# Layer 1 of two fused attention layers in two phases: raw scores kept in SBUF with a running maximum

## The reference

```python
# layer 0: 64 inner channels, no scale
f = einsum('bni,bim->bnm', theta_x, phi_x)
y = einsum('bnm,bmi->bni', softmax(f), g_x)
x = W_w @ y + W_b + x
# layer 1: 128 channels, scale 1/sqrt(128)
attn = softmax(einsum('bnc,bcm->bnm', q, k) * scale)
x = x + einsum('bnm,bmc->bnc', attn, v)
```

## Time and profile before

| | |
|---|---|
| median of three runs | 3430.94 us (3430.82 to 3434.11) |
| the profiled execution | 3435.51 us, its span 3433.7 us, mean granted clock 0.989 |
| busy, share of the span | PE 97%, POOL 86%, DVE 61%, ACT 49% |
| a steady block of layer 0 | 44.0 us |
| a steady block of layer 1 | 59.9 us |

### The profile page before, as it was taken

How to read it: one execution, slowest core, us unless ns; L and a number is a source line. 1 busy time by engine, 2 the same in 40 slices (tenths; PEclk the granted TensorE clock), 3 DMA queues, 4 the chain that set the end, 5 groups by cost and what they waited for, 6 DMA issues and landing times.

```text
span 3433.7 us, 46684 instructions
## 1 busy us (share of the span) xinstructions
PE 3336.5 (97%) x13124; PEld 2113.4 (62%) x13124; DVE 2100.6 (61%) x3029; ACT 1671.5 (49%) x2241; POOL 2965.9 (86%) x1366
## 2 busy tenths in 40 slices
PE   6999999999999989999999998999999999999998
PEld 4555566666655556666655555666665555566665
DVE  4555576776555557676755555677675555666674
ACT  4455445444455544444445554544454555444444
POOL 4999699898989969898989996989898999688897
PEclk9999999999999999999999999999999999999999
DMA  1000000000000000000000000000000000000000
GB/s 43 13 18 19 28 10 22 12 22 16 19 19 16 19 23 16 16 19 19 13 19 19 19 16 23 19 13 21 16 19 13 19 19 16 19 13 16 13 13 10
DMA packets 34038, 61.73 MB, mean 18 GB/s; under 512 B 5280, under 2 KB 5920, under 8 KB 33568
## 3 DMA queue, kind: packets, MB, share of 16 engines
q1 hardware_dynamic: 33824, 59.23, 5.6%
HBM read 42.44 MB, written 16.78 MB: 17 GB/s over the span
## 4 chain that ended last, share of the span: by engine, by line
PE 91%; DVE 3%; issue 2%; POOL 2%; ACT 1%; SPq 0%; DVEq 0%; DMA 0%; ACTq 0%; POOLq 0%
PE acc_out L471 16%; PE rough L398 15%; PE acc_out L455 13%; PE scores L420 7%; PE scores L423 7%; PE scores L425 7%; PE scores L429 7%; PE scores L426 7%; PE acc_out L443 2%; PE acc_out L441 2%; PE acc_out L442 2%; DVE piece_max L793 2%; PE rough L380 2%; PE acc_out L492 1%; PE acc_out L386 1%
## 5 line engine op out<-in xcount | busy, mean ns | idle before, releaser
L280 POOL TENSOR_TENSOR sums<-sums,probs 128x1024 f32<-128x1024 f32 x886 | 2116.0, 2388 | 145.1 <-ACT probs L718 104.7
L793 DVE TENSOR_REDUCE piece_max<-rough 128x1 f32<-128x512 f32 x2024 | 1309.5, 684 | 649.1 <-PE rough L398 646.2
L810 DVE TENSOR_TENSOR probs<-scores,shift_rows 128x1024 f32<-128x1024 f32 x512 | 626.7, 1224 | 567.3 <-PE scores L429 543.2
L718 ACT ACTIVATE probs<-scores 128x1024 f32<-128x1024 f32 x512 | 520.1, 1025 | 672.8 <-PE scores L423 665.1
L711 ACT ACTIVATE probs<-probs 128x1024 f32<-128x1024 f32 x512 | 539.4, 1053 | 499.6 <-DVE probs L810 499.4
L914 POOL TENSOR_TENSOR p_lo<-probs,p_hi 128x1024 fp32r<-128x1024 f32 x192 | 459.2, 2392 | 188.0 <-ACT probs L711 187.7
L471 PE MATMUL acc_out<-probs,v_vals 128*128 128x512 f32 x1280 | 605.4, 595 | 0.0
L425 PE MATMUL scores<-qry_a,k_hi 128*128 128x512 f32 x1024 | 507.8, 496 | 0.0
L455 PE MATMUL acc_out<-probs,g_vals 128*64 128x512 f32 x2048 | 495.0, 605 | 0.0
L420 PE MATMUL scores<-qry_a,phi_a 128*128 128x512 f32 x1024 | 432.3, 422 | 0.0
L710 ACT ACTIVATE p_hi<-probs 128x1024 fp32r<-128x1024 f32 x192 | 203.3, 1059 | 441.0 <-DVE probs L810 397.2
(11 more groups left out here) (97 smaller groups left out, 2961.0 us busy)
## 6 DMA issues: line engine op xcount, KB each, us to landing
x_q<-x SPq DMA_DIRECT2D x32, 256.0 KB, 2.7
x_res<-x SPq DMA_DIRECT2D x32, 256.0 KB, 3.0
mid<-mid_new SPq DMA_DIRECT2D x32, 256.0 KB, 2.2
x_q<-mid SPq DMA_DIRECT2D x32, 256.0 KB, 2.7
x_res<-mid SPq DMA_DIRECT2D x32, 256.0 KB, 3.2
out<-result SPq DMA_DIRECT2D x32, 256.0 KB, 2.3
x_kv<-x SPq DMA_DIRECT2D x24, 256.0 KB, 2.7
probs<-x SPq DMA_DIRECT2D x2, 1024.0 KB, 6.0
```

The source lines that it names most:

```text
L280: eng.tensor_tensor(sums[:, parity], sums[:, parity], probs[:, s % P_BUFS], ALU.add).then_inc(s_plus, 1)
L793: nc.vector.reduce_max(piece_max[:, t, c:c + 1], src, AX.X).then_inc(s_reduced, 1)
L810: nc.vector.tensor_tensor(probs[:, s % P_BUFS].rearrange("p (h c) -> p h c", c=QB), scores[:, s % 2].rearrange("p (h c) -> p h c", c=QB), ...
```

## The change

- Layer 1 has no pieces any more. While block i's values are multiplied, TensorE computes the full raw scores of block i+1 (`raw_group`). For each group VectorE takes a running maximum over the groups (`max_raw`), and ScalarE copies the group to SBUF (`copy_raw`, 16 buffers of `bufs`). At the end VectorE folds the two halves of the running maximum (`top`), four float32 matmuls with the identity turn it (`turn_max`), VectorE reduces it and makes the diagonal (`raw_diagonal`), and one matmul spreads it into a bank of `rough` (`raw_row`). In the next block VectorE adds this row to the stored scores (`shift_scores`, now from SBUF with the row in PSUM) into one of 4 rotating buffers, and ScalarE takes the exponential as before.
- All 16 groups of values of layer 1 are full float32; `HALVED`, `p_hi`, `p_lo`, `v_hi`, `v_lo` and what makes them are gone.
- Layer 0's last block takes the raw scores of groups 0 to 13 of layer 1's first block instead of pieces, two steps behind, all through the one buffer `rough`; the turn does groups 14 and 15. Layer 1's last block takes the pieces for the next image's layer 0, now through the four banks of `scores`.
- In both layers the denominator is one float32 matmul of ones with the sums, which gives it spread over the rows; VectorE inverts that in place in four instructions of 128 x 128 at steps 6 to 9. The columns, their two parts, the eight diagonals and the two matmuls are gone.
- `q_whole`, `result`, the second `sums`, `diag` and `shift_rows` are given up for room: the whole query goes through `whole` like keys and `phi`, with more waits on its users (`l_q`, `l_k`, `l_phi`), and outputs go through `mid_new`. In layer 1 the next query is projected at step 13 into the free bank instead of at step 14 into `rough`.

```diff
 P_BUFS = 8
+ROT = 4
...
+RECIP_AT = (6, 7, 8, 9)
+NORM_AT = 9
...
+RAW_LAG = 2
+RAW_Q_AT = 13
...
+        def probs_free(eng, layer, g, s):
+            n = ROT if layer == 1 else P_BUFS
+            eng.wait_ge(s_used, g * GROUPS + s + 1 + P_BUFS - n)
+            eng.wait_ge(s_plus, added(g, s - n) if s >= n else added(g - 1, GROUPS + s - n))
...
+        def raw_bank(st, s):
+            if st.layer == 1:
+                return scores[:, s % 2]
+            return rough[:] if s < GROUPS - 1 else scores[:, 0]
...
+            def raw_group(st, s):
+                n, g, parity = st.raw_nth, st.g + 1, 1 - st.parity
+                if s == 0:
+                    pe.wait_ge(h_q, g + 1)
+                if st.turn:
+                    if s == 0:
+                        pe.wait_ge(s_reduced, (st.nth + 1) * PIECES + 1)
                     else:
-                        mm(place, k_hi[:, k], qa, start=True, stop=False)
-                        mm(place, k_lo[:, k], qa, start=False, stop=False)
-                        if s == 0 and h == 0:
-                            pe.wait_ge(l_q, g + 1)
-                        last = mm(place, k_hi[:, k], qb, start=False, stop=True)
-                last.then_inc(s_scores, 1)
-            def halved_values(b, g, nth, parity, s):
-                pe.wait_ge(s_p_lo, halved(nth, s))
-                pe.wait_ge(l_v, (b + 1) * BLOCKS)
-                n = HALVED.index(s) % 2
+                        pe.wait_ge(s_copied, copied(n, s - 1))
+                    if s % 2 == 0:
+                        pe.wait_ge(s_k_hi, n + s // 2 + 1)
+                elif st.prev is None and s < 2:
+                    pe.wait_ge(s_copied, copied(n - 1, GROUPS - 1))
+                    if s == 1:
+                        pe.wait_ge(h_v, (st.b + 1) * BLOCKS)
+                else:
+                    pe.wait_ge(s_copied, copied(n, s - 2))
+                bank = raw_bank(st, s)
                 for h in range(TPG):
-                    hi = v_hi[:, s // TPG, h * KT:(h + 1) * KT]
-                    lo = v_lo[:, s // TPG, h * KT:(h + 1) * KT]
-                    at = slice(h * QB, (h + 1) * QB)
-                    mm(acc_out[:, parity], hi, p_hi[:, n, at], start=False, stop=False)
-                    mm(acc_out[:, parity], hi, p_lo[:, n, at], start=False, stop=False)
-                    last = mm(acc_out[:, parity], lo, p_hi[:, n, at], start=False, stop=False)
-                last.then_inc(s_used, 1)
-            def value_batch(g, parity, first):
+                    k = slice((s * TPG + h) * KT, (s * TPG + h + 1) * KT)
+                    place = bank[:, h * QB:(h + 1) * QB]
+                    mm(place, k_hi[:, k], qry_a[:, parity], start=True, stop=False)
+                    if st.turn and s % 2 == 0 and h == 0:
+                        pe.wait_ge(l_k, n + s // 2 + 2)
+                    mm(place, k_lo[:, k], qry_a[:, parity], start=False, stop=False)
+                    if s == 0 and h == 0:
+                        pe.wait_ge(l_q, g + 1)
+                    last = mm(place, k_hi[:, k], qry_b[:, parity], start=False, stop=True)
+                last.then_inc(s_raw, 1)
+            def turn_max(n, g, parity):
+                pe.wait_ge(s_topped, n + 1)
+                pe.wait_ge(s_done, g + 1)
+                for t in range(SUB):
+                    last = mm(acc_out[:, parity, t * P:(t + 1) * P], run_max[:, t * P:(t + 1) * P], idt[:],
+                              start=True, stop=True)
+                last.then_inc(s_turned, 1)
+            def raw_row(g, parity):
+                pe.wait_ge(s_diag, g + 1)
+                mm(row_bank(parity), ones_r[:], diag[:], start=True, stop=True).then_inc(s_row, 1)
...
+                mm(acc_out[:, parity], ones, total[:], start=True, stop=True).then_inc(s_den, 1)
...
+                for s in range(GROUPS):
+                    if st.layer == 0:
+                        if s == 0 and st.prev == 1:
+                            pe.wait_ge(h_g, (st.b + 1) * BLOCKS)
+                        pieces_first = s > 0 and s % BATCH != BATCH_AT
+                        if pieces_first:
+                            two_pieces(s)
+                        score_group(st.prev, st.g, st.nth, st.parity, s)
+                        if not pieces_first:
+                            two_pieces(s)
+                        if st.turn and s >= RAW_LAG:
+                            raw_group(st, s - RAW_LAG)
+                        around(s)
+                        values(st, s)
+                        third_piece(s)
+                    else:
+                        values(st, s)
+                        if s == 1 and st.prev == 1:
+                            raw_row(st.g, st.parity)
+                        if st.raw:
+                            raw_group(st, s)
+                        two_pieces(s)
+                        if s == 0 and st.prev == 1:
+                            turn_max(st.nth, st.g, st.parity)
+                        around(s)
+                        third_piece(s)
...
+                    if st.layer == 1 and s == RAW_Q_AT and st.next_q:
+                        pe.wait_ge(s_done, st.g + 2)
+                        if st.phi_g:
+                            pe.wait_ge(h_g, (st.b + 1) * BLOCKS + st.i + 1)
+                        next_queries(st.g + 2, st.next_q[0], free_bank)
+                    if st.layer == 0 and s == NEXT_Q_AT and st.next_q:
                         pe.wait_ge(s_reduced, st.pieces + PIECES + 1)
                         next_queries(st.g + 2, st.next_q[0], two_banks(1))
                 if st.ends:
...
+            def turn(st):
+                pe.wait_ge(s_done, st.g + 3)
+                for s in range(GROUPS - RAW_LAG, GROUPS):
+                    raw_group(st, s)
+                project_keys(scores[:, 1, QB:GC], wt_v, mid_new[:, st.parity], p_v)
+                turn_max(st.raw_nth, st.g + 1, 1 - st.parity)
+                raw_row(st.g + 1, 1 - st.parity)
...
+            def make_k(n, c, src, splits):
                 act.wait_ge(l_k, n + 1)
                 copy(cols(k_hi, c), src, K_B, K_S).then_inc(s_k_hi, 1)
+                act.wait_ge(l_q, splits)
                 copy(whole[:], src, K_B, K_S).then_inc(h_k, 1)
...
+            def copy_raw(st, s):
+                act.wait_ge(s_maxed, maxed(st.raw_nth, s))
+                act.wait_ge(s_shifted, shifted(st.raw_nth - 1, s))
+                if st.turn and s >= GROUPS - (P_BUFS - ROT):
+                    probs_free(act, 1, st.g, s)
+                copy(bufs[:, s], raw_bank(st, s)).then_inc(s_copied, 1)
...
+                        if st.turn and s >= RAW_LAG:
+                            copy_raw(st, s - RAW_LAG)
+                    else:
+                        if st.raw and s == 0:
+                            copy_raw(st, s)
+                        probs_shifted(st.nth, s)
+                        if st.raw and s > 0:
+                            copy_raw(st, s)
+                        if s == RAW_Q_AT + 1 and st.next_q:
...
+            def max_raw(st, s):
+                n = st.raw_nth
+                dve.wait_ge(s_raw, copied(n, s))
+                if s == 0:
+                    nc.vector.tensor_copy(run_max[:], raw_bank(st, s)).then_inc(s_maxed, 1)
+                    return
+                dve.wait_ge(s_maxed, maxed(n, s - 1))
+                nc.vector.tensor_tensor(run_max[:], raw_bank(st, s), run_max[:], ALU.max).then_inc(s_maxed, 1)
+            def top(n):
+                dve.wait_ge(s_maxed, maxed(n, GROUPS - 1))
+                nc.vector.tensor_tensor(run_max[:, 0:QB], run_max[:, 0:QB], run_max[:, QB:GC],
+                                        ALU.max).then_inc(s_topped, 1)
+            def raw_diagonal(n, g, parity):
+                dve.wait_ge(s_turned, n + 1)
+                diagonal(g, row_bank(parity)[:, 0:SUB], acc_out[:, parity].rearrange("p (t c) -> p t c", c=P))
...
+                dve.wait_ge(s_copied, copied(nth, s))
+                probs_free(dve, 1, g, s)
+                dve.wait_ge(s_row, g + 1)
                 nc.vector.tensor_tensor(
-                    probs[:, s % P_BUFS].rearrange("p (h c) -> p h c", c=QB),
-                    scores[:, s % 2].rearrange("p (h c) -> p h c", c=QB),
-                    shift_rows[:, parity].unsqueeze(1).to_broadcast([P, TPG, QB]), ALU.add).then_inc(s_shifted, 1)
-            def reciprocals(g, parity):
+                    prob(1, s).rearrange("p (h c) -> p h c", c=QB),
+                    bufs[:, s].rearrange("p (h c) -> p h c", c=QB),
+                    row_bank(parity).unsqueeze(1).to_broadcast([P, TPG, QB]), ALU.add).then_inc(s_shifted, 1)
...
+            def reciprocal(g, parity, t):
                 dve.wait_ge(s_den, g + 2)
-                den = acc_out[:, parity, 0:2 * SUB].rearrange("p (t c) -> p t c", c=2)[:, :, 0:1]
-                rcol = acc_out[:, parity, 2 * SUB:3 * SUB]
```

(26 more changed lines are left out.)

416 lines of the change are left out of this document (171 added, 245 removed).

## The result

The changed kernel takes 3449.27 us in the median of five runs (3447.76 to 3449.67) against 3434.11 (3430.82 to 3436.33) of the kernel before: a ratio of 1.0045, with a 95% interval of 1.003 to 1.006. It is slower by 0.45%, and the forecast was 3419, faster by 0.35%.

A forecast was written before the change was run, and what follows sets the result against it. TensorE, busy 97% of the span, was taken as the bound, with only the turn a chain. Terms +89 +36 -20 -45 -27 -30 -15 +0 gave -12 us on a median of 3430.9: 3419 us, forecast range 3395 to 3445.

The forecast's parts named there:

- layer 0's last block and the turn, 4: Raw groups through one buffer make TensorE wait, +89 us; the turn's chain grows 8.9 each, +36 for four.
- layer 1's first block, 4: Block after the turn: lighter TensorE sum, with waits and low clock 53.1 us instead of 58.1, -20 for four.
- steady layer 1 blocks, 18: Blocks 1 to 6 of three images: TensorE 54.1 plus 3.3 us of waits, 57.4 against 59.9, -45.
- six blocks of the last image: Layer 1 without `phi` and `g`: 53.1 us a block against 58.3, of which -27 was credited.
- the very last block: Only values left, POOL's 13 additions after the boundary, then the tail: about 52 us against 67, -15.
- Layer 0, 28 ordinary blocks ... 0: Ordinary layer 0 blocks: VectorE gets 4.0 us more at steps 6 to 9, removed rows pay for the waits, 0.
- Last block of layer 1 ... -30: In three images, pieces without raw groups: VectorE becomes the bound, some 49.5 us against 59.5, -30.
- A: Rival: waits are smaller and TensorE's sums alone count, 3317 us in full, 3368 for half; chance 0.17.
- B: Rival: reciprocals on VectorE at steps 6 to 9 decide, slower, 3438 or 3461 to 3475 us; chance 0.23.
- C: Rival: the turn costs another 10 us each as TensorE stays longer at 1.2 GHz, 3459 us; chance 0.10.

The follow-up runs named there:

- e4_cheap: Changed kernel with the four 128x128 reciprocals replaced by in-place copies, so the output is not divided: 3399.73 us.
- f6_best: Changed kernel with raw groups by halves, 512-wide maximum without the last fold, later phi, later layer 1 finish, earlier query at the seam, one turn wait less: 3316.09 us.
- f2_hand: e1_halves with layer 1's finish at step 11 of layer 0's first block and the query copied earlier in layer 1's last block: 3360.41 us.
- e3_recip_alone: Kernel before with only the new denominator matmul and four 128x128 reciprocals at steps 6 to 9: 3438.23 us, 1.0012 of before.
- e1_halves: Changed kernel with each raw group signalled, maximized, copied and waited for by halves of 512 columns: 3369.22 us, 0.9812 of before.
- f3_phi: e1_halves with phi multiplied behind step 10's values in layer 1 and taken by ScalarE ahead of the raw copy: 3348.13 us.
- e2_q_ahead: Changed kernel with ScalarE's two next-query copies moved ahead of step 14's exponential and raw copy in layer 1: 3480.06 us, 1.0135 of before.
- f5_notop: e1_halves with a running maximum 512 wide instead of 1024, so that the last fold, `top`, is gone: 3355.02 us.

## Why the prediction was wrong

| term of the sum | forecast | measured |
|---|---|---|
| layer 0's last block and the turn, 4 | +89 +36 = +125 | +134 |
| layer 1's first block, 4 | -20 | -31 |
| steady layer 1 blocks, 18 | -45 | -35 |
| six blocks of the last image | -27 | -31 |
| layer 1's last block, 3 | -30 | -21 |
| the very last block | -15 | -14 |
| layer 0's first block after layer 1, 3 | 0 | +10 |
| the rest | 0 | +2 |
| sum | -12 | +14 |

Measured is profile against profile, 3447.8 and 3433.7 us of span. The mechanisms of the larger terms were there: the alternating wait behind the single buffer, the waits for finish and for `phi` in steady blocks and the one at the boundary, VectorE as the busiest engine of layer 1's last block, layer 0's ordinary blocks at 44.1. The first four over TensorE's whole run, waits by releaser (us, times, longest):

```profile
PE rough L464 <- ACT bufs L687: 39.4, 28, 1.6
PE acc_out L400 <- DVE mid_new L918: 28.6, 21, 3.2
PE scores L464 <- ACT bufs L687: 28.1, 32, 2.7
PE acc_out L406 <- ACT phi_a L688: 25.7, 21, 1.2
```

The forecast of -12 was a small difference of terms of over 100, and the result is 26 us above it. Four terms came out 9 or 10 us too low each, and two the other way by 11 and 4. What failed falls in three parts: low clock at the seams from layer 1 to layer 0, which stood at nothing (10 us), the order of the queues at the same seams (about 8), and the units for TensorE's own steps (up to 19, the first and third row).

**Low clock at the seams from layer 1 to layer 0.** The prediction counted the low clock for the turn alone. The kernel before has a granted clock of 1.00 in layer 1's last block and the layer 0 block after it, with 0.2 us of waits for TensorE in the former. The changed kernel has two stretches of 3.4 us at half clock at each of the three seams:

```profile
1744.40:1747.81 3.41, 3.41 (x5) 1.35 (x4) 2.81 (x4) 1.63 (x2) 1.68 (x1) 0.50 0.54 154
1764.88:1768.29 3.41, 3.41 (x7) 1.66 (x6) 1.29 (x2) 1.02 (x1) 3.33 (x3) 0.50 0.01 2
```

The first begins 0.5 us after TensorE had waited 3.2 us for finish (L400), the second 1.0 us after the later of two waits, of 1.7 and 0.5 us, for the query's copies. e4_cheap prices a stretch at 1.6 us in either block, so six of them are 10 us of the 26; this is an estimate from that kernel, and no run takes the low clock alone out of the changed one. f6_best, where TensorE waits 1.8 us for finish and under 0.5 for the query's first copy, has no such stretch. What decides where one falls is not shown.

**The units of TensorE's own steps** (layer 0's last block and the turn, steady layer 1 blocks). The waits came out nearly as counted: 10.0 us in layer 0's last block (10.8 forecast), 2.8 in a steady one (3.3). The rest of the block, which is TensorE's own work, did not: 57.0 for 53.6, and 55.1 for 54.1. In this trace a single-pass matmul pushes the next by 0.23 us when another such stood right before it; the first after a wait, and the first after float32 matmuls without any wait, push it by 0.34:

```profile
1231.77 1.03 PE L496 MATMUL acc_out<-bufs,g_vals 128*64 128x512 f32 x4
1232.73 0.50 PE L436 MATMUL scores<-qry_a,phi_a 128*128 128x512 f32 x1
1233.07 0.39 PE L439 MATMUL scores<-qry_b,phi_b 128*128 128x512 f32 x1
1233.30 0.40 PE L436 MATMUL scores<-qry_a,phi_a 128*128 128x512 f32 x1
```

So a raw group behind a wait and ahead of values takes 1.59 us and not the 1.38 of the sum, and a score group behind values 1.03 and not 0.93. The block and turn came to 33.6 us more each and not 31.3, and layer 1's steady block to 58.0, not 57.4. A wait in the trace begins at a matmul's modelled end, 0.16 us beyond its step of 0.23, so each wait reads that much too short and the work too long; by steps the waits of that block are 11.1 us.

**The step "Layer 0, 28 ordinary blocks ... 0".** It took the three blocks that follow layer 1 for ordinary. There layer 1's finish stands at step 9 too, behind the fourth reciprocal and the multiply, and the pieces behind all three. The chain at the handover, start and the time on the chain:

```profile
1761.45 0.67 ACT whole L688
1762.11 0.59 ACT qry_a L688
1762.75 0.51 PE acc_out L424
1763.28 0.60 ACT qry_b L687
...
1790.64 1.30 DVE piece_max L839 x3
...
1792.46 0.97 DVE acc_out L892
1793.45 0.71 DVE acc_out L899
1794.52 0.07 DVE mid_new L918
...
1795.19 1.29 DVE piece_max L839 x2
```

From 1790.64 to 1796.48 the chain is VectorE's alone: three reductions (1.30 of their time on it), reciprocal, multiply, finish, two reductions, while TensorE's pieces wait. f2_hand, with the finish two steps later, is 1.0 us shorter, and e3_recip_alone 0.9 longer by the early one. Of the 3.3 us, 0.9 are this and 1.6 the low clock; the rest holds TensorE's wait for the query's second copy (0.45, the fourth row).

**The step "Last block of layer 1 ... -30".** It forecast 49.5 us, measured 52.8. The row's matmul (L424) waits for `h_q`, so for ScalarE's copies of the query, and these stand behind the exponential of step 14, which comes after VectorE's diagonal and shift: at 1761.45 to 1762.75, in the upper rows, one chain that ran through three engines and that the step did not name. TensorE waits 1.7 us for it, and f2_hand got 1.7 back in this block. With the 1.6 of low clock that is the 3.3. f6_best, which has neither, takes 49.6.

**`top` was priced at 0.6.** It took 0.97 in most blocks, and TensorE waited for it 5.5 us in the whole run; it is a small part of the error, but of the later kernels' time a large one (22 to 32 us of waits in e1_halves, f3_phi and e2_q_ahead).

**The other way**, layer 1's first block was 49.9 and not 53.1: 3.5 us had been put on it for the low clock. The turn, longer now, took that stretch (mean granted clock 0.73 over the turn, 1.00 in the block behind it). The turn's length was forecast well, 24.8 us against 25.4. A part of its chain:

```profile
1298.05 1.25 POOL k_lo L993
...
1300.14 0.43 PE rough L470
1300.57 0.43 PE rough L464
...
1301.97 1.24 DVE run_max L865
...
1308.80 0.70 DVE run_max L870
```

Here the raw group has steps of 0.43 us (L470 and L464), nearly twice the 0.23 of the block behind it: 1.2 GHz, after 10 us in which TensorE had only the denominator and the output projection to do.

The rivals: A (only the sums count) fails on 58.0 us and on the 67.0. B, by which it would be slower, was not the way: reciprocals of 0.95 us left layer 0's ordinary blocks at 44.1 (e3_recip_alone). C named the low clock, but in the turn, where it cost less than counted (turn and first block 75.3 us, forecast 77.9); it cost 10 us at the other seam. The direction was missed by small terms that no rival held together.

## What to carry to other kernels

Work taken off the bounding engine is worth its price only if what replaces it is handed on in time: a result that two engines read in turn needs its buffer split to the bank, so that the chain runs at the grain of half a tile; this alone was worth 80 us here, more than the whole change was to bring. Walk the seams (first and last block of each stage) step by step like the steady block, for queue orders meet there that do not meet elsewhere, and look at the granted clock there, for waits that are new to TensorE came with stretches at half clock. And when a forecast is a small difference of large terms, the sign is not known, whatever the care in each.

## What the runs showed of the hardware

- An addition or maximum on VectorE with both operands in SBUF, 128x512, takes 0.69 us when free and 0.97, 2.75 or 2.90 when GpSimd had started an instruction that reads SBUF; it ends 0.54 to 0.55 us after that one. f5_notop, which leaves it out, is 14 us faster than e1_halves. A move of 0.6 us in GpSimd's schedule (e2_q_ahead) cost 31 us by it.
- The first single-pass matmul of 512 columns after a wait of TensorE pushes the next by 0.34 us, and so does the first after float32 matmuls without a wait (1232.73 in the changed kernel); a steady one by 0.23.
- A stretch of 3.4 us at half clock in a busy block cost 1.6 us (e4_cheap, one seam against another). The kernel before had none at the seams from layer 1 to layer 0, the changed one two at each.
- The reciprocal of 128x128 takes 0.95 us, four in a row 3.40 (the turn of the changed kernel): 0.85 each.
- Whether ScalarE and VectorE could read one bank of PSUM at the same time, so that copy and maximum run side by side, was not tried.
